# One transformer layer on one core: a batch's side work moved to other steps between its score tiles

## What is computed

```python
q, k, v = heads(x @ qkv_w.T)                        # 16 heads of 16
q, k = q * cos + rot(q) * sin, k * cos + rot(k) * sin
w = softmax(q @ k.T / 4 + alibi)                    # 512 x 512 per head
x = layernorm(x + (w @ v) @ proj_w.T + proj_b)
shared = silu(x @ sW1 + sb1) @ sW2 + sb2
combine = top2(sqrt(softplus(x @ routing_W.T + expert_bias)))
routed = sum_e combine[e] * (silu(x @ rW1[e] + rb1[e]) @ rW2[e] + rb2[e])
x = layernorm(x + shared + routed)
```

## Time and profile before

| what | value |
|---|---|
| median of 3 runs | 1660.95 us (1656.72 to 1667.56) |
| the profiled execution | 1663.59 us, span 1661.8 us |
| TensorE matmuls busy | 1458.4 us, 88% of the span |
| VectorE, ScalarE, GpSimd busy | 1171.7, 1019.3, 723.9 us |
| mean granted TensorE clock | 0.936 of full speed |
| DMA | 242 MB, mean 146 GB/s |

### The profile page before, as it was taken

One profiled execution on the slowest core, in us unless ns is written; L12 is line 12 of the kernel. 1 busy time (PEld: TensorE's weight loads), 2 busy tenths in 40 slices (PEclk: granted clock), 3 DMA queues, 4 the chain that ended last, 5 costly groups with the idle time before them and its releaser, 6 DMA issues.

```text
span 1661.8 us, 33130 instructions
## 1 busy us (share of the span) xinstructions
PE 1458.4 (88%) x11110; PEld 801.2 (48%) x11110; DVE 1171.7 (71%) x2631; ACT 1019.3 (61%) x1742; POOL 723.9 (44%) x655
## 2 busy tenths in 40 slices
PE   7987999999999889899999899988888999896467
PEld 4433444444444435555555544454455555564345
DVE  7665777878778787666666677857776577645674
ACT  1465666666767656666677576666566587675242
POOL 2233353635545343541535253533666344255630
PEclk8789899999999989999999999999999899998789
DMA  7334243434343324454545433443566566686531
GB/s 208 115 109 147 91 124 101 129 108 132 102 123 116 115 92 141 132 175 139 178 138 165 130 120 116 128 139 120 166 214 222 177 217 209 192 257 212 168 106 51
DMA packets 185349, 242.00 MB, mean 146 GB/s; under 512 B 67239, under 2 KB 104190, under 8 KB 185182
## 3 DMA queue, kind: packets, MB, share of 16 engines
q1 hardware_dynamic: 154746, 181.18, 36.4%
q0 software_dynamic: 10752, 29.37, 5.4%
q10 hardware_dynamic: 19684, 29.33, 5.0%
HBM read 152.53 MB, written 91.44 MB: 147 GB/s over the span
## 4 chain that ended last, share of the span: by engine, by line
PE 51%; DVE 15%; SPq 14%; DMA 10%; issue 6%; POOL 2%; ACT 2%; POOLq 0%; ACTq 0%; DVEq 0%
PE pS L641 15%; PE pV L683 9%; PE pG L707 6%; DVE negm L932 5%; PE pG L729 3%; PE pG L716 3%; SPq L390 2%; DMA xg<-d_x 2%; PE pS L647 2%; DMA d_rec<-scr 2%; PE pG L810 2%; SPq L459 2%; PE pG L818 2%; SPq L499 1%; DMA d_sum<-pvs 1%
## 5 line engine op out<-in xcount | busy, mean ns | idle before, releaser
L932 DVE TENSOR_REDUCE negm<-pS 128x1 f32<-128x512 f32 x1024 | 659.6, 683 | 336.4 <-PE pS L647 329.6
L1368 ACT ACTIVATE ee<-pT,slp 128x512 f32<-128x512 f32 x1024 | 649.0, 684 | 216.8 <-PE pT L668 215.2
L641 PE MATMUL pS<-ka,qa 62*128 62x512 f32 x1024 | 485.4, 509 | 81.0 <-DVE negm L932 68.3
L662 PE MATMUL pT<-qa,ka 64*128 64x512 f32 x1024 | 480.9, 504 | 0.2 <-ACT ee L1368 0.2
L641 PEld LDWEIGHTS pS<-ka,qa 62*128 62x128 f32 x1024 | 198.4, 194 | 330.0 <-issue 312.8
L683 PE MATMUL pV<-ee,vv 128*32 128x512 f32 (+1 forms) x2048 | 286.8, 633 | 0.0
L647 PE MATMUL pS<-mAB,tri 64*128 64x64 bf16 x2048 | 243.6, 200 | 0.0
L668 PE MATMUL pT<-mAB,tri 64*128 64x64 bf16 x2048 | 239.9, 198 | 0.0
L1555 POOL TENSOR_TENSOR raw<-raw,rope 128x512 f32<-128x512 f32 x61 | 78.2, 1282 | 330.0 <-DVE sh L966 329.9
L662 PEld LDWEIGHTS pT<-qa,ka 64*128 64x128 f32 x1024 | 195.6, 191 | 4.5 <-issue 3.1
L647 PEld LDWEIGHTS pS<-mAB,tri 64*128 64x128 bf16 x2048 | 119.8, 99 | 139.6 <-issue 107.3
(11 more groups left out here) (186 smaller groups left out, 2192.8 us busy)
## 6 DMA issues: line engine op xcount, KB each, us to landing
d_part<-parts SPq DMA_DIRECT2D x63, 512.0 KB, 2.8
qa<-d_part SPq DMA_DIRECT2D x378, 64.0 KB
wb<-in_wb SPq DMA_DIRECT2D x77, 256.5 KB
xg<-d_x SPq DMA_DIRECT2D x77, 256.0 KB, 2.9
d_y<-yb ACTq DMA_DIRECT2D x77, 256.0 KB, 2.6
ka<-d_part SPq DMA_DIRECT2D x128, 128.0 KB
xT<-in_xT SPq DMA_DIRECT2D x16, 512.0 KB
ka<-d_part SPq DMA_DIRECT2D x128, 64.0 KB
```

The costliest lines, as they stand in the source:

```text
L641: e.matmul(pS[:, k, :], qa[g % 4][r, i, t * 128:t * 128 + 128].bitcast(F32R), ka[g % 4][r, i, :].bitcast(F32R), start=True, stop=False)
L662: e.matmul(pT[:, k, :], ka[g % 4][r, i, kt * 128:kt * 128 + 128].bitcast(F32R), qa[g % 4][r, i, :].bitcast(F32R), start=True, stop=False)
L932: e.tensor_reduce(negm[:, g % 2, j, t + k:t + k + 1], pS[:, k, :], AX, ALU.max, negate=True).then_inc(s_max, 1)
L1368: e.activation(ee[:, k, d % 7, :], pT[:, k, :], ACT.Exp, scale=slp[:, 6, h:h + 1]).then_inc(s_exp, 1)
```

## The change

Only constants differ. No instruction is added to a batch or taken from it; the warm-up alone grows by ten matmuls.

```diff
-SHUFFLE = (2, 2, 2, 2)
-ROPE = (1, 1, 1, 3, 3)
-PARTS_OUT = 5
-V = ((10, 12), (15, 17))
+SHUFFLE = (2, 2, 2, 6)
+ROPE = (1, 1, 1, 2, 2)
+PARTS_OUT = 4
+V = ((2, 3), (5, 11))
 XT_LOAD = -41
-X_LOAD = 43
-ASSEMBLE = -6
-M_SPLIT, M_OUT, M_IN = (-1, -1, 2)
+X_LOAD = 40
+ASSEMBLE = -4
+M_SPLIT, M_OUT, M_IN = (-1, 0, 3)
 EVAC = 24
-SUMS_OUT, SUMS_IN, RECIP, REC_OUT, REC_IN, SCALE = (2, 2, 5, 5, 6, 8)
+SUMS_OUT, SUMS_IN, RECIP, REC_OUT, REC_IN, SCALE = (2, 2, 5, 5, 5, 8)
 PAIR = 11
-BIASX = 55
-PROJ = ((58, 61), (65, 65))
+BIASX = 59
+PROJ = ((61, 61), (62, 65))
 RESIDUAL = (61, 65)
-RANK = 77
+RANK = 76
 PLACE = 77
-SCATTER = (78, 79, 80, 81, 82, 83, 84, 85)
-UP = (77, 78)
-GATE = 83
-DOWN = (87, 89)
-BASE_OUT = 93
+SCATTER = (78, 79, 80, 81, 82, 83, 84, 84)
+UP = (76, 77)
+GATE = 85
+DOWN = (87, 87)
+BASE_OUT = 100
-LAST_EXPS, LAST_SOFTPLUS, LAST_POW = (78, (80, 81), 85)
+LAST_EXPS, LAST_SOFTPLUS, LAST_POW = (76, (77, 81), 86)
-BLOCKS_AT = ((90, 4.0, 25, 250, 4.0), (92, 2.0, 27, 146, 3.0), (92, 1.0, 11, 103, 2.0))
+BLOCKS_AT = ((90, 4.0, 25, 250, 4.0), (92, 2.0, 27, 146, 3.0), (92, 1.0, 11, 104, 3.0))
-LOADD, GATED, DOWND = (-5, 1, 2)
-WEIGHTS, VAR3, NORM3, OUTD = (0, 24, 25, 27)
+LOADD, GATED, DOWND = (-6, 1, 2)
+WEIGHTS, VAR3, NORM3, OUTD = (-1, 21, 23, 24)
-LATE, PREP, PADS = 11, (18, 20, 22, 24), 40
-WARM = (5, 6, 4, 4, 5)
+LATE, PREP, PADS = (6, (18, 20, 20, 22), 38)
+WARM = (6, 9, 6, 6, 7)
```

## The result

The changed kernel took 1681.2 us (1675.46 to 1685.82) beside 1659.0 of the kernel before: a ratio of 1.0132, interval 1.0102 to 1.0162, slower by 22 us where 46 less were forecast. Its profiled execution took 1680.45 us, span 1678.6.

What follows compares the result with a forecast made beforehand. Time was taken as near the sum over steps of the longest engine, mostly TensorE; 17.6 - 10.4 + 22 + 5 + 5 + 2 + 3 + 1 + 1 = 46.2 us less than 1660.95 gave 1615, forecast 1600 to 1626 (chance 0.36), range 1588 to 1648.

Steps and rivals of the forecast that it cites:

- the part on SyncE's queue: SyncE's issue order: the block load issues about 5.6 us earlier, ahead of ASSEMBLE; 22 us plus 5 us less.
- ASSEMBLE: Its move two steps later ends eight xg waits (17.1 us) and the half clock behind them; 22 us less, bounds 8 and 29.
- rival B: Max rows read later; if a landing takes 3.5 us, half a microsecond lost at 60 octets, 1645 us; chance 0.13.
- A: Rival: bases wait for GpSimd's scatters near step 24, 5 us in each of 14 batches, 1674 us; chance 0.08.
- The 5 us more from batch 13 on: Batches 13 to 15 and tail: 5 us taken of the other 21.6 us of xg waits, bounds 0 to 15.
- Quiet batches: Batches without routed blocks: 2.2 us less each, 17.6 us for batches 1 to 6, 11 and 12.
- steps 26 to 12: Moved projection and value groups fill TensorE's waits in these nineteen steps: 44.45 us to 43.1, 1.3 less.
- steps 13 to 25: Fewer groups at 13 to 22, but TensorE stands about 2.0 us at 25 for scatters: 30.55 to 29.7, 0.9 less.
- the 10.4 taken off: A half-clock stretch expected behind the new 2 us stall at step 25: 1.3 us in eight batches, set against the gain.
- rival D: Clock stays full in quiet batches and the scatter wait is small, 4.2 us a batch kept, 1589 us; chance 0.16.
- Batch 13 and the turn: The projection's wait for batch 13's pair sum goes, 5 us; a value group covers the turn's norm wait, 2 us.
- Batch 1, WARM, tail: Earlier loads and pads in batch 1, 3 us less (bounds -4 and 8); longer warm-up 1; bias in the tail 1.

Runs made afterwards that it cites:

- queue_mix: The changed kernel with M_OUT, M_IN, BASE_OUT and X_LOAD put back as in the kernel before; ratio 0.9944 to the kernel before.
- assemble_again: The kernel before with only the constant ASSEMBLE moved from -6 to -4, a second run of that edit; ratio 0.9883.
- assemble_compute_again: The kernel before with ASSEMBLE at -4 and values, projection, bias, rank, up, gate, down and scatter moved, run in the fourth group; ratio 0.9929.
- the fourth group's intervals: Runs on the kernel before, same session: ASSEMBLE at -4 alone, 0.9837 to 0.9930; with all moved computation, 0.9905 to 0.9953.
- the fifth group's pair: The kernel before with ASSEMBLE at -4 and the start's constants (LATE, PREP, PADS, WARM), with and without the moved computation; ratios 1.0007 and 0.9906.
- assemble_and_compute: The kernel before with ASSEMBLE at -4 and values, projection, bias, rank, up, gate, down and scatter moved, run in the third group; ratio 0.9994.

## Why the prediction was wrong

*The step that failed* is the part on SyncE's queue. It followed one move, ASSEMBLE's, through the queue and put the others at nothing without a reason: X_LOAD and BASE_OUT were never costed, and M_IN only as lateness of the max rows (rival B), not as what its going does to the sums behind it. My reading of the landing, "1.8 us for the sums", was of an octet in which 2.6 us of small reads lay in front. That is a property of the order, and the change removed the order. In its place the runs showed round trips of SyncE that wait for the bytes sent ahead of them, with the block batches and the rest waiting for SyncE's later loads. They put 1.9% on it (queue_mix against the changed kernel), some 31 us, the larger part by the max rows. Rival B came nearest: it named the right constant and asked what happens if the sums' landing takes 3.5 us (the mean round trip was 3.3), but the wait it drew from this, of the turned tiles for max rows, came only in batch 1. That its price was 30 us is luck. A, the one on the slower side, did not happen: steps 24 and 25 took 4.88 us together, with TensorE idle for 0.79, where the scatters were to cost 2.0.

*ASSEMBLE* was right where it was reasoned out: 22 us forecast for batches 7 to 12 and 17 and 18 measured, and the eight xg waits went to one of 0.6. The 5 us more from batch 13 on did not come. In all 27 were forecast and 1.2%, some 19.5, measured. In the changed kernel the gain was there but covered: TensorE's waits from 552 to 1099 us show 8.0 us for xg, and the keys' parts, absent before from that stretch's list, took their place, since the queue was late for everything:

```profile
PE pS L641 <- DMA ka<-d_part: 16.6, 10, 3.8
PE pG L802 <- DMA xg<-d_x: 8.0, 7, 2.1
```

*Quiet batches* were right in size (2.2 us a batch forecast, 2.1 measured in batch 4, no half clock at step 4, steps 29 and 30 as priced), but in part by luck: steps 26 to 12 gave 0.4 us instead of 1.3, since step 1 took 2.47 us instead of 1.96 and step 5 2.95 instead of 2.65, and steps 13 to 25 gave 1.7 instead of 0.9. The stall at steps 24 and 25 was short and brought no half clock (granted 1.00), so that the 10.4 taken off was not due. The second step that failed is the sum over batches: eight times a quiet batch was entered as a gain of the whole, while batch 0, at the lower clock, and the batches with blocks were entered at nothing. In the profiles of assemble_again and assemble_compute_again they take it back: 5.6 and 5.0 us against a gain of 6.3.

*The clock.* Both conditions of rival D came in batch 4, the full clock and a small scatter wait, but the batch gained 2.1 us and not D's 4.2.

*Batch 13 and the turn*: the projection's wait went, the turn's fell from 7.5 to 4.1 (2 us forecast), and the projection's wait in the tail from 24.3 to 20.8 (1 forecast). Batch 13 still took 109.1 us instead of 103.1, and 106.6 with the max rows back, so the queue outweighed it.

*Batch 1, WARM, tail*: 5 us of gain forecast, none that the ratios can tell, batch 1 of the wrong sign (3 less forecast, 4.1 more measured), just outside my bounds. The first pair came 1.1 us later, where WARM was allowed 0.8. I had moved the pads two steps earlier as a gain; what follows them in the queue was not asked.

By ratios, each term the difference of two measured kernels: ASSEMBLE -1.2% (assemble_again), the computation +0.5 (assemble_compute_again), the rest (parts, reciprocals, shuffle, start and tail) +0.15, too little to tell from nothing (from there to queue_mix), the max rows with the two large transfers +1.9 (from there to the changed kernel); together +1.3. Such a chain always adds up; what it gives is the size of the terms. Set beside the forecast, the 68 us between 46 less and 22 more are about 31 of SyncE's order, 22 of the computation (14 less forecast for quiet batches, clock, pair sum and turn, 8 more measured), 8 of ASSEMBLE and 7 of the start and tail.

What stays open: how the 1.9% divides in the tail of the run (batches 13 to 15 and tail, +19.6 us), where blocks and experts load at every second step and the lower clock has its part; and whether the half per cent of the computation is real (the fourth group's intervals overlap, the fifth group's pair gives 1.0%). No run issues the round trips from another engine's queue.

## What to carry to other kernels

When an engine issues a DMA and then waits for it before issuing the next, its queue is a serial resource, and here the price of that wait rose with the bytes that the same queue had just sent. Put small issues, not large ones, ahead of a round trip, and cost every moved DMA by what then stands behind it. Price a move in each kind of stretch (start at low clock, quiet, loaded), not by the quiet one times a count; and try a bundle's strongest term alone: here it beat the bundle by 2.5%.

## What the hardware showed unexpectedly

A round trip of a small DMA took 1.74 us behind small reads, 2.62 behind a block load (512 KB in two), 5.17 and 5.23 with the large ones above ahead, and 8.1 behind the pads and the parts. Rival B had asked about 3.5. The rows behind a block load, of the kernel before:

```profile
769.76 0.34 SPq L474 DMA_DIRECT2D d_rec<-scr  x1
772.38 1.73 SPq L484 DMA_DIRECT2D rb<-d_rec  x4
```

One block load ahead is thus not what makes the 5 us; more bytes are: in the kernel before too, with x and a block load, 1 MB, issued in the 3.4 us ahead, a round trip took 4.40 (890.32 to 894.72).

The kernel before took 1662 to 1664 us in three groups of runs and 1677 in two, and all six kernels profiled in those two have waits of VectorE and ScalarE whose releaser the trace calls remote, absent in all the fourteen others. So VectorE's waits of assemble_and_compute:

```profile
DVE negm L932 <- remote: 31.2, 12, 4.9
```

The same source as assemble_compute_again has no such line. What releases them is not known; only one core runs. It is not the chip: the record has one chip for the first and the third group, and one for the fourth and the fifth. The stalls are why the third and fifth groups carry no small term here.
